# A four-layer graph network: the fourth layer's masks are made as bytes during the third layer's sweep and kept in memory

## What is computed

```python
def _L2_gnn_ref(x, adj, W, a):                      # third layer, 2 heads of 128
    adj = adj + jnp.eye(n, dtype=adj.dtype)
    scores = jax.nn.leaky_relu(e1[:, :, None] + e2[:, None, :], negative_slope=ALPHA)
    scores = jnp.where(adj > 0, scores, jnp.asarray(NEG_INF, scores.dtype))
    attn = jax.nn.softmax(scores, axis=-1)
    h_prime = jnp.einsum('hij,hjo->hio', attn, xt)
def _L3_gnn_ref(x, adj, W, a_src, a_dst, bias):     # fourth layer, 4 heads of 64
    e = jax.nn.leaky_relu(s_src[:, None, :] + s_dst[None, :, :], NEG_SLOPE)
    e = jnp.where((adj > 0.5)[:, :, None], e, MASK_VAL)
    alpha = jax.nn.softmax(e, axis=0)
    out = jnp.einsum('ijh,ihc->jhc', alpha, h).reshape(n, HEADS * C) + bias
```

## Time and profile before

| what | us |
|---|---|
| median of three runs | 2545.11 |
| lowest and highest of them | 2538.03, 2555.68 |
| the profiled execution, its own time | 2537.44 |
| its span in the trace | 2535.7 |
| TensorE busy in it | 2096.0 |
| VectorE busy | 1616.5 |
| ScalarE busy | 710.3 |
| GpSimd busy | 247.4 |

### The profile page before, as it was taken

The page is one execution under the profiler, slowest core; times in us unless marked ns, Lnnn a source line. Parts: engine busy times, 40 slices in busy tenths (PEclk is TensorE's granted clock), DMA queues, the critical chain, the costliest instruction groups (busy, mean ns, idle before and its releaser), DMA issues. The chain is left out here.

```text
span 2535.7 us, 25288 instructions
## 1 busy us (share of the span) xinstructions
PE 2096.0 (83%) x9643; PEld 1127.8 (44%) x9652; DVE 1616.5 (64%) x2562; ACT 710.3 (28%) x969; POOL 247.4 (10%) x130
## 2 busy tenths in 40 slices
PE   4979999149999989997899939997799654999991
PEld 2545556013343433346555414455799641222230
DVE  3334445468686767643477763434788657989888
ACT  0112222268686868754222200001000020000000
POOL 0000000000000000000000000000000005656540
PEclk9989999569999999999999969999899877999995
DMA  4355554434454545336100024440100104323211
GB/s 127 118 198 184 183 198 144 171 117 169 156 183 147 180 142 189 122 121 196 42 1 0 1 67 134 133 118 14 47 15 17 56 1 168 95 82 94 62 54 44
DMA packets 132529, 271.83 MB, mean 107 GB/s; under 512 B 14486, under 2 KB 45048, under 8 KB 128544
## 3 DMA queue, kind: packets, MB, share of 16 engines
q1 hardware_dynamic: 114080, 240.84, 29.7%
q10 hardware_dynamic: 18324, 29.34, 3.2%
HBM read 226.76 MB, written 43.37 MB: 107 GB/s over the span
## 5 line engine op out<-in xcount | busy, mean ns | idle before, releaser
L761 PE MATMUL banks<-arena 128*128 128x512 f32 (+1 forms) x1512 | 597.8, 552 | 57.5 <-DVE arena L1328 54.6
L761 PEld LDWEIGHTS banks<-arena 128*128 128x128 f32 x1512 | 270.1, 192 | 383.6 <-issue 376.0
L1545 DVE SCALAR_TENSOR_TENSOR arena<-arena 128x1024 f32<-128x1024 f32 (+3 forms) x264 | 324.2, 1301 | 24.6 <-PE banks L893 13.8
L1328 DVE TENSOR_TENSOR arena<-arena 128x1536 f32<-128x1536 f32 (+2 forms) x132 | 201.3, 1526 | 156.7 <-ACT arena L1008 156.7
L822 PE MATMUL banks<-arena 128*128 128x512 f32 (+2 forms) x528 | 209.4, 548 | 44.5 <-DVE arena L1420 43.8
L719 PE MATMUL banks<-arena 128*128 128x512 f32 (+2 forms) x528 | 240.6, 580 | 0.0
L884 PE MATMUL banks<-arena 128*64 128x512 f32 (+3 forms) x1056 | 223.3, 561 | 12.9 <-DVE arena L1545 12.9
L859 PE MATMUL banks<-arena 128*124 128x129 f32 (+2 forms) x1936 | 217.8, 275 | 13.7 <-DVE arena L1502 13.7
L859 PEld LDWEIGHTS banks<-arena 128*124 128x124 f32 (+2 forms) x1936 | 216.1, 187 | 15.5 <-issue 12.6
L628 POOL TENSOR_SCALAR arena<-arena 128x1024 bf16<-128x1024 f32 (+1 forms) x66 | 209.2, 3171 | 132.1 <-DVE arena L1545 124.2
L1001 ACT ACTIVATE arena<-arena 128x512 f32<-128x512 f32 (+2 forms) x264 | 162.7, 662 | 143.1 <-PE banks L761 137.0
(11 more groups left out here) (177 smaller groups left out, 1937.0 us busy)
## 6 DMA issues: line engine op xcount, KB each, us to landing
arena<-adj_T SPq DMA_DIRECT2D x210, 256.0 KB, 3.0
arena<-hw_rows SPq DMA_DIRECT2D x126, 384.0 KB, 3.1
arena<-in_adj SPq DMA_DIRECT2D x21, 1354.0 KB
adj_T<-arena ACTq DMA_DIRECT2D x105, 256.0 KB, 2.2
arena<-in_adj SPq DMA_DIRECT2D x25, 1024.0 KB
arena<-in_adj SPq DMA_DIRECT2D x42, 512.0 KB
hw_rows<-arena SPq DMA_DIRECT2D x1, 8064.0 KB
arena<-in_adj SPq DMA_DIRECT2D x21, 330.0 KB
```

The costliest lines, as they stand in the source:

```text
L761: ins = PE.matmul(bank(2 * (c % 2) + f)[:, 0:wid(c)], hs[0:R, m % 3, h * D + f * P:h * D + (f + 1) * P], E[0:R, n % 3, h, 0:wid(c)], start ...
L1328: V.tensor_tensor(e, e, a, ALU.mult).then_inc(s["p_ok"], 1)
L1545: V.scalar_tensor_tensor(PM3[0:k, n % 2, h, 0:w], r3_bc[0:k, h, c * WW:c * WW + w], smalls[0:k, 4, h * T + t:h * T + t + 1], mask3[0:k, n ...
```

## The change

During the third layer's sweep GpSimd compares each of the 22 rows of tiles, all 2708 columns in one instruction, with 0.5 and writes bytes. SP loads the rows of `adj` for it into `rows3` (two buffers in `tmp2`) and stores the bytes from `bytes3` (two buffers in `wcat0`) to the new DRAM tensor `mask3_rows`. SP does that in 23 turns, four ahead of each chunk's wait for its heads (three ahead of the last chunk's); in a turn it loads row t once mask t-2 is made, and stores mask t-1. In the fourth layer the strips that SP loads are these bytes (four buffers instead of three), VectorE reads them directly and waits for the DMA, and GpSimd's loop is gone. The stage end of the third layer's sweep now also waits for the last byte stores.

```diff
+        rows3 = tmp2.rearrange("p t d -> p (t d)")[:, 0:2 * N].rearrange("p (q n) -> p q n", q=2)
+        bytes3 = wcat0.rearrange("p k n -> p (k n)")[:, 0:2 * N // 4].bitcast(U8).rearrange("p (q n) -> p q n", q=2)
...
-        strips3 = sb(3, WW)
-        mask3 = sb(3, WW, dt=BF16)
+        mask3 = sb(4, WW, dt=U8)
...
         def strip3(sp, n):
             c, t = divmod(n, T)
-            if n >= 3:
-                sp.wait_ge(l3_mask, n - 2)
-            load(sp, strips3[0:kp(t), n % 3, 0:wide(c)], adj[t * R:t * R + kp(t), c * WW:c * WW + wide(c)], l3_in[n % 3])
+            if n >= 4:
+                sp.wait_ge(l3_p, H3 * (n - 3))
+            load(sp, mask3[0:kp(t), n % 4, 0:wide(c)], mask3_rows[t * R:t * R + kp(t), c * WW:c * WW + wide(c)], l3_in[n % 4])
+
+        def mask_rows(sp, t):
+            if t < T:
+                if t >= 2:
+                    sp.wait_ge(m3_made, t - 1)
+                load(sp, rows3[0:kp(t), t % 2, :], adj[t * R:t * R + kp(t), :], m3_in[t % 2])
+            if t >= 1:
+                u = t - 1
+                sp.wait_ge(m3_made, t)
+                load(sp, mask3_rows[u * R:u * R + kp(u), :], bytes3[0:kp(u), u % 2, :], m3_out[u % 2])
...
+            turns = iter(range(T + 1))
             for c in range(CH):
+                for t in itertools.islice(turns, 4):
+                    mask_rows(sp, t)
                 sp.wait_ge(l2_heads, H2 * sum(len(blocks2(i)) for i in range(c + 1)))
...
+            for q in range(2):
+                sp.wait_ge(m3_out[q], 16 * len(range(q, T, 2)))
             sp.wait_ge(h2_out, 16 * outs)
...
             maxima(0, H2)
+            for t in range(T):
+                pool.wait_ge(m3_in[t % 2], 16 * (t // 2 + 1))
+                if t >= 2:
+                    pool.wait_ge(m3_out[t % 2], 16 * (t // 2))
+                G.tensor_scalar(bytes3[0:kp(t), t % 2, :], rows3[0:kp(t), t % 2, :], 0.5, None, ALU.is_gt).then_inc(m3_made, 1)
...
-            for n in range(UNITS3):
-                c, t = divmod(n, T)
-                pool.wait_ge(l3_in[n % 3], 16 * (n // 3 + 1))
-                if n >= 3:
-                    pool.wait_ge(l3_p, H3 * (n - 2))
-                G.tensor_scalar(mask3[0:kp(t), n % 3, 0:wide(c)], strips3[0:kp(t), n % 3, 0:wide(c)], 0.5, None, ALU.is_gt
-                                ).then_inc(l3_mask, 1)
...
-                dve.wait_ge(l3_mask, n + 1)
+                dve.wait_ge(l3_in[n % 4], 16 * (n // 4 + 1))
                 for h in range(H3):
                     V.scalar_tensor_tensor(PM3[0:k, n % 2, h, 0:w], r3_bc[0:k, h, c * WW:c * WW + w],
-                                           smalls[0:k, 4, h * T + t:h * T + t + 1], mask3[0:k, n % 3, 0:w],
+                                           smalls[0:k, 4, h * T + t:h * T + t + 1], mask3[0:k, n % 4, 0:w],
```

More of the change, by code:

```diff
@@ L3 @@
+import itertools
 from contextlib import ExitStack, contextmanager
@@ L134, in build @@
     adj_T = nc.dram_tensor("adj_T", (N, N), F32).ap()
+    mask3_rows = nc.dram_tensor("mask3_rows", (N, N), U8).ap()
     hw_rows = nc.dram_tensor("hw_rows", (N, H0 * D), F32).ap()
@@ L310, in build @@
         l2_scaled, l2_p, l2_mm, l2_read, l2_heads = (sem(f"l2_{s}") for s in ("scaled", "p", "mm", "read", "heads"))
-        l3_in = [sem(f"l3_in{i}") for i in range(3)]
-        l3_mask, l3_g, l3_scaled, l3_p, l3_mm, l3_read = (sem(f"l3_{s}") for s in ("mask", "g", "scaled", "p", "mm", "read"))
+        m3_in, m3_out = ([sem(f"m3_{s}{i}") for i in range(2)] for s in ("in", "out"))
+        m3_made = sem("m3_made")
+        l3_in = [sem(f"l3_in{i}") for i in range(4)]
+        l3_g, l3_scaled, l3_p, l3_mm, l3_read = (sem(f"l3_{s}") for s in ("g", "scaled", "p", "mm", "read"))
         b_in, b_diag, b_rowfree, b_negm, b_exp = (sem(f"b_{s}") for s in ("in", "diag", "rowfree", "negm", "exp"))
```

## The result

The changed kernel takes 2658.64 us (median of four runs, 2653.24 to 2668.22) against 2550.39 for the kernel before beside it (four runs, 2538.03 to 2558.36). The ratio is 1.0409, with a 95% interval of 1.0374 to 1.0444: slower by 4.1%, where the prediction expected a change of less than 1%.

What follows compares the result with a forecast made beforehand. TensorE was taken to bound the third layer's sweep (1.76 us a unit), VectorE's 5.56 us over TensorE's 5.438 the fourth's. 2537.44 - 2.6 - 5.2 + 9 = 2538.6, put on the runs' median 2546 us; range 2532 to 2575.

Steps and rivals of the forecast that it cites:

- Fourth layer, steady part, -2.6 us: Fourth layer's sweep: without GpSimd's masks VectorE's slow products go and units fall from 5.56 to TensorE's 5.438 us, -2.6 us.
- Its start, -5.2: Fourth layer's start: no wait for GpSimd's first mask, TensorE starts at about 2123.7 instead of 2128.84, -5.2 us.
- GpSimd's rows at 7.5 + 0.3 us, output as bytes at no extra price: Third layer's sweep: 22 GpSimd operations of 7.5 us plus 0.3 waiting, bytes counted like bf16, 172 of 220 us.
- Rival 2: Third layer: byte output is dear for GpSimd; +40 us at 1.5 times the price, +119 at twice; chance 0.08.
- rival 3: Fourth layer: TensorE's 5.438 us only echoes VectorE's pace, units fall to 4.78, total 2504 us; chance 0.07.
- The hold: Third layer's sweep: each 2708-element GpSimd row holds VectorE up once, by 2.2 us, made good in five units.
- rival 1: Third layer: long GpSimd rows hold VectorE throughout, +118 us (about 2655), or +76 in its second form; chance 0.10.
- 5.6 us a row, 123 - 47 = +76: Rival 1's second form: hold of 0.78 us, then for the part beyond 1024; 123 us less VectorE's slack of 47.
- The third layer's end, +9 with stalls and tail: Third layer's end: about 5 us of stalls, then last rows queued ahead of chunk 5's heads; +9 us, ends +3.5 and +20.
- the forecast of 1.2 us: Whole kernel: sum of -2.6, -5.2 and +9 on 2537.44 us gives +1.2 us; chance 0.70.

Runs made afterwards that it cites:

- cut at 1536: The changed kernel with each row compared by two GpSimd instructions, of 1536 and 1172 columns, instead of one: 2646.09 us.
- cut at 2048: The changed kernel with each row compared by two GpSimd instructions, of 2048 and 660 columns, instead of one: 2609.3 us.
- the kernel with three cuts: The changed kernel with each row compared by three GpSimd instructions (1024, 1024, 660 columns) instead of one: 2562.36 us, ratio 1.0025 to the kernel before.

## Why the prediction was wrong

*Fourth layer, steady part, -2.6 us*: right. VectorE's slow products are gone and TensorE's 5.438 and 3.617 hold to the ends of the chunks. *Its start, -5.2*: right. TensorE's first matmul comes 28.8 us behind the drain before it, and it was 34.5, so 5.7 sooner (VectorE's first product 5.0: 26.3 against 31.3). That leaves -3.0 for the rest of the sweep, against -2.6. Together -8.7 against -7.8.

*GpSimd's rows at 7.5 + 0.3 us, output as bytes at no extra price*: right, 7.16 us in the mean, with a pause of 0.26 to 1.0 us inside a batch ahead of every second row and none ahead of the others; a piece of 1024 or 660 costs what it costs with bf16. Rival 2 falls with it, and rival 3 with TensorE's 5.438.

*The hold, "0.78 + 1684 x 0.83 ns (the slope from 660 to 1024 ...) = 2.2 us"*: this step failed. It measured 5.7. The slope came from two lengths that lie at and under 1024, and was carried on to 2708, two and a half times as far. Between 1024 and 1172 elements there is a step of about 1.9 us, which the run cut at 1536 shows, and past 2048 a second one; the slope sees nothing of them. The supporting row was the wrong one too. The product behind the copy L620 took 2.64 us, a hold of 2.1. But the copy's record, 8.01 us from 2100.65, runs beside a VectorE product until 2106.3 and ends at 2108.66, so the copy itself seems to work for only some 2.4 us, and the hold fills nearly all of that. A comparison of the same length works for 7.0. Read as a share of the working time, the row spoke for the long hold. The prediction knew that its hold stood at the edge (2.1 us a row), named the mechanism that took place, in rival 1, whose second form has "5.6 us a row", and gave it 1 in 10. The edge should have made that chance larger: a forecast in which one term hangs on an extrapolation, and which tips over a few tenths of a us further on, isn't a forecast at 7 in 10.

*"5.6 us a row, 123 - 47 = +76"*: the hold is right, and the arithmetic is not. It set the slack of the whole sweep against the holds. The slack outside a batch of rows can't be used, because the three buffers let VectorE no further ahead than three units; that is the calculation with the 64 missing units. With the holds as the traces sum them up (the products' records less the 180.6 us that they take in the kernel before) it can be checked in three kernels; 1.29 us makes a unit's products, 1.76 is TensorE's unit:

| kernel | GpSimd's rows, us | held in all, us | missing units | us from them | measured, us |
|---|---|---|---|---|---|
| changed | 157.4 | 122.3 | 62 | 110 | 112.3 |
| cut at 1536 | 167.2 | 114.7 | 54 | 96 | 98.0 |
| cut at 2048 | 161.8 | 79.6 | 28 | 50 | 53.3 |

It is 2 to 4 us short in all three. Each of them has the clock at 1.2 GHz for part of the sweep (86, 70 and 39 us; about 5 before), which the calculation leaves out.

*The third layer's end, +9 with stalls and tail*: in the changed kernel itself there is no tail (85.5 against 85.4), because the sweep that the heads come from is later still. In the kernel with three cuts, where a row's holds come to about what I had thought (at most 0.84 a piece of 1024, 2.0 a row), there is one: +7.7 in the sweep and +5.6 behind it, 13.3 where the prediction took 9, between 3.5 and 20. So had the row been cut, the forecast of 1.2 us would have met 4.7.

## What to carry to other kernels

A duration is only known between the lengths that the trace has; where the sum tips on a longer one, the chance goes to the other side, or the instruction is cut to a length that is known. Where VectorE makes two-input products, GpSimd's comparisons are kept to 1024 elements, which took the change here from 4.1% slower to 0.25%, or ScalarE makes them. Slack counts only while the engine that has it is free to use it, and taking work from an engine earns no more than its excess over the next bound, here 5.56 over 5.438 us.

## What the runs showed of the hardware that was not expected

The hold on a two-input VectorE instruction is a staircase in GpSimd's length: 0.48 us at 660 elements, 0.78 at 1024, 2.64 at 1172, 3.41 at 2048, 5.72 at 2708. A one-input comparison of 128x512 float32 to bytes is held for nearly the whole GpSimd instruction, 6.8 of 7.03 us, where the two-input product is let go after 5.7. What is left of GpSimd's instruction after the hold repeats with 1024 elements: 1.32 us for 660 and for 2708, 1.93 for 1024 and for 2048. A GpSimd fill of 2708 bytes a partition takes 2.35 us and holds nobody. When TensorE is fed late in batches, its clock falls to 1.2 GHz again and again (86 of the sweep's 332 us, from VectorE's first product on), and for some us after each batch it is the slower for it. And a sweep of the first layer, which no version touches, has two lengths about 18 us apart, which is more than the change gains in the fourth layer; what decides between them stays open.
